# Where routing steps stand inside the slots of a two-layer hybrid block, and how the last rows are sent to their experts

## What is computed

```python
x = x + attention(layernorm(x))   # q = elu(x Wq)+1, k = elu(x Wk)+1, v = x Wv, H = 64
                                  # S_t = S_{t-1} + k_t v_t^T ; z_t = z_{t-1} + k_t
                                  # o_t = S_t^T q_t / max(z_t.q_t, 1e-6) ; out = o Wo
x = x + ffn(layernorm(x))
x = x + mix(layernorm(x))         # prev_t = x_{t-1} + d prev_{t-1}, d = exp(-exp(decay))
                                  # out = sigmoid(r_in Wr^T) * ((v_in Wv^T) Wo^T), *_in from x and prev
x = x + ffn(layernorm(x))

def ffn(x):                       # 8 experts, 128 -> 512 -> 128, the best one per token
    probs = softmax(x @ router_W + router_b)
    e = argmax(probs)
    return probs[e] * (relu(x @ W1[e] + b1[e]) @ W2[e] + b2[e])
```

## Time and profile before

| | |
|---|---|
| median of three runs | 393.11 us (392.72 to 397.33) |
| the profiled execution | 397.11 us, of which the span of the trace is 395.2 us |
| granted TensorE clock, mean | 0.862 of full speed |
| attention slots, first expert stage | about 27 to 94 us, about 98 to 203 us |
| mix slots, second expert stage | about 203 to 285 us, about 285 to 386 us |
| TensorE, VectorE, POOL, ScalarE busy | 75%, 63%, 51%, 37% |

### The profile page before, as it was taken

The page is one execution under the profiler, slowest core; times in us unless marked ns, Lnnn a source line. Parts: engine busy times, 40 slices in busy tenths (PEclk is TensorE's granted clock), DMA queues, the critical chain, the costliest instruction groups (busy, mean ns, idle before and its releaser), DMA issues.

```text
span 395.2 us, 8901 instructions
## 1 busy us (share of the span) xinstructions
PE 296.7 (75%) x2097; PEld 258.3 (65%) x2097; DVE 250.0 (63%) x996; ACT 147.1 (37%) x413; POOL 201.3 (51%) x259
## 2 busy tenths in 40 slices
PE   2899999680599379999923989695089729999980
PEld 1367666450488279999912878574088629999980
DVE  4656788784388167877725579467248627777760
ACT  3545554211133024444414555724123203444430
POOL 5823517777345724555424152777734554445550
PEclk9999999986589669999985889977559957999996
DMA  7990000024446448876325000001645736877700
GB/s 206 240 165 4 1 2 28 29 56 141 118 129 178 108 113 221 218 209 191 81 76 138 2 0 2 27 27 43 169 136 148 186 66 179 227 205 199 188 19 0
DMA packets 42609, 44.21 MB, mean 112 GB/s; under 512 B 7120, under 2 KB 29905, under 8 KB 42560
## 3 DMA queue, kind: packets, MB, share of 16 engines
q10 hardware_dynamic: 11808, 20.71, 20.9%
q1 hardware_dynamic: 26176, 14.39, 15.7%
q0 software_dynamic: 4576, 8.54, 6.1%
HBM read 33.06 MB, written 11.53 MB: 113 GB/s over the span
## 4 chain that ended last, share of the span: by engine, by line
PE 38%; issue 27%; DVE 11%; SPq 7%; another core or an unknown queue 5%; POOL 5%; ACT 2%; DMA 2%; DVEq 1%; POOLq 0%; ACTq 0%
PE pair L1319 14%; PE pair L1305 11%; PE bank L1305 4%; PE pair L1246 2%; POOL sorted L453 2%; DVE hT L1017 2%; SPq L344 2%; PE pair L1247 2%; SPq L340 2%; PE pair L1264 2%; SPq L312 1%; DVE xsn L1001 1%; ACT xn L535 1%; DVEq L1006 1%
## 5 line engine op out<-in xcount | busy, mean ns | idle before, releaser
L1319 PE MATMUL pair<-w2s,hT 128*128 x624 | 89.0, 289 | 8.2 <-issue 7.6
L1319 PEld LDWEIGHTS pair<-w2s,hT 128*128 128x128 f32 x624 | 80.9, 203 | 10.4 <-issue 9.9
L453 POOL DMA_INDIRECT sorted<-rows,place x64 | 64.2, 1003 | 31.3 <-issue 17.8
L1305 PE MATMUL pair<-xsT,w1s 128*128 128x128 f32 x472 | 70.2, 288 | 0.8 <-issue 0.8
L1305 PEld LDWEIGHTS pair<-xsT,w1s 128*128 128x128 f32 x472 | 63.6, 205 | 1.2 <-issue 1.2
L459 POOL DMA_INDIRECT out<-ys,xs x39 | 38.0, 975 | 41.2 <-issue 26.4
L459 POOL DMA_INDIRECT x_mid<-ys,xs x39 | 38.0, 975 | 40.7 <-issue 23.4
L1017 DVE TENSOR_SCALAR hT<-pair,w1s 128x128 f32<-128x128 f32 x156 | 47.1, 343 | 8.6 <-remote 3.9
L1028 DVE SCALAR_TENSOR_TENSOR ys<-pair,xs 128x128 f32<-128x128 f32 x78 | 27.2, 349 | 25.7 <-remote 13.0
L1009 DVE SCALAR_TENSOR_TENSOR xs<-b2b,xs 128x128 f32<-128x128 f32 x78 | 27.4, 352 | 21.4 <-DVE xsn L1001 14.6
L646 ACT COPY xsT<-bank 128x128 f32<-128x128 f32 x40 | 10.6, 265 | 67.4 <-PE bank L1296 27.4
(11 more groups left out here) (160 smaller groups left out, 505.5 us busy)
## 6 DMA issues: line engine op xcount, KB each, us to landing
w1s<-in_L_ffn_W_b ACTq DMA_DIRECT2D x78, 258.0 KB
xs<-sorted SPq DMA_DIRECT2D x78, 66.0 KB
rows<-in_L_attn_a_x SPq DMA_DIRECT2D x8, 256.0 KB, 4.9
w2s<-in_L_ffn_W SPq DMA_DIRECT2D x8, 256.0 KB, 5.5
rows<-x_mid SPq DMA_DIRECT2D x8, 256.0 KB, 4.8
sorted<-pad SPq DMA_DIRECT2D x30, 66.0 KB, 3.5
sorted<-rows,place POOLq DMA_INDIRECT x64
x_mid<-ys,xs POOLq DMA_INDIRECT x39
```

What stands on the lines that cost most here:

```text
L453: pool.indirect_dma_start(sorted_rows[l], bass.IndirectOffsetOnAxis(ap=place[:, t:t + 1], axis=0), rows[:, t, :], None).then_inc(s_sent[l] ...
L1305: mm = nc.tensor.matmul(bank[2 + 2 * half + i % 2][:, c * P:(c + 1) * P], w1s[i % NW][:, f:f + P], xsT[i % NB][:], start=True, stop=True)
L1319: mm = nc.tensor.matmul(bank[6 + i % 2][:, 0:P], hT[i % NB][:, c], w2s[:, bass.ds(e, 1), c, :].rearrange("p o d -> p (o d)"), start=(c == ...
```

## The change

The routing steps are the same instructions, in another order. In the attention slots VectorE does the places right after the mask instead of after the state, and the choice in front of the moments; POOL does the old logits in the middle of a group's four sends; ScalarE's exponentials move to the end of the slot. In the mix slots VectorE does places and choice in front of the moments, ScalarE's exponentials come at the end of the slot, a slot earlier (one more table load there), and TensorE counts in front of logits and mix. In the expert stages the last batch is chosen, counted and tabled earlier (2, 4, 5), and its eight sends are issued one per slot, behind the scatters of slots 4 to 11, instead of all after one scatter.

```diff
@@ -32,7 +32,7 @@
 
 STAGES = [(1, 9), (3, 8), (4, 22)]
 
-CHOOSE_AT, COUNT_AT, TABLE_AT = 3, 6, 6
+CHOOSE_AT, COUNT_AT, TABLE_AT = 2, 4, 5
 
 
 def after(eng, sem, n):
@@ -442,16 +442,24 @@
                 nc.gpsimd.tensor_tensor(lold[:, tiles(g)], kv[g % 2][:, :, H:VC], per_tile(std1[:, tiles(g)], GT),
                                         ALU.mult).then_inc(AS["lold"], 1)
 
-            def send(l, S, g):
-
+            def rows_ready(l, S, g):
                 b = batch_of(ROUTE_BATCHES, g)
                 pool.wait_ge(S["xnew"], g + 1)
                 pool.wait_ge(S["rs2"], 3 * (b + 1))
                 pool.wait_ge(s_gate[l], 2 * (b + 1))
                 pool.wait_ge(S["place"], b + 1)
-                for t in range(g * GT, (g + 1) * GT):
-                    pool.indirect_dma_start(sorted_rows[l], bass.IndirectOffsetOnAxis(ap=place[:, t:t + 1], axis=0),
-                                            rows[:, t, :], None).then_inc(s_sent[l][stage_of_batch(b)], 16)
+
+            def send_tile(l, t):
+                b = batch_of(ROUTE_BATCHES, t // GT)
+                pool.indirect_dma_start(sorted_rows[l], bass.IndirectOffsetOnAxis(ap=place[:, t:t + 1], axis=0),
+                                        rows[:, t, :], None).then_inc(s_sent[l][stage_of_batch(b)], 16)
+
+            def send(l, S, g, half=None):
+
+                if half != 1:
+                    rows_ready(l, S, g)
+                for t in range(g * GT + (GT // 2 if half == 1 else 0), (g + 1) * GT - (GT // 2 if half == 0 else 0)):
+                    send_tile(l, t)
 
             def scatter(l, i):
                 b = i % ND
@@ -462,11 +470,14 @@
                                         ).then_inc(s_sct[b], 16)
 
             def experts(l):
+                late = [t for g in ROUTE_BATCHES[LASTB] for t in range(g * GT, (g + 1) * GT)]
                 for i in range(ST):
                     scatter(l, i)
-                    if i == COUNT_AT - 1:
-                        for g in ROUTE_BATCHES[LASTB]:
-                            send(l, (AS, BS)[l], g)
+
+                    if i == COUNT_AT:
+                        rows_ready(l, (AS, BS)[l], LASTG)
+                    if COUNT_AT <= i < COUNT_AT + len(late):
+                        send_tile(l, late[i - COUNT_AT])
 
             def first_indirect():
 
@@ -487,9 +498,11 @@
                 if 0 <= k - 1 < NG:
                     z_dot_q(k - 1)
                 if k - 5 >= 0:
-                    send(0, AS, k - 5)
+                    send(0, AS, k - 5, 0)
                 if 0 <= k - 1 < NG:
                     old_logits(k - 1)
+                if k - 5 >= 0:
+                    send(0, AS, k - 5, 1)
             send(0, AS, 4)
             send(0, AS, 5)
             row_scales(AS, LASTB)
@@ -597,8 +610,6 @@
                 if k == NG:
                     for i in range(NW // 2):
                         load_w1(0, i)
-                if (b := batch_ending(ROUTE_BATCHES, k - 4)) is not None and b < LASTB - 1:
-                    lexp(0, AS, b)
                 if k + 1 < NG:
                     evac_xT(AS, k + 1, "vp")
                 if k + 2 < NG:
@@ -607,8 +618,8 @@
                     evac_v(k)
                 if 0 <= k - 1 < NG:
                     evac_o(k - 1)
-                if k == NG:
-                    lexp(0, AS, LASTB - 1)
+                if (b := batch_ending(ROUTE_BATCHES, k - 3)) is not None and b < LASTB:
+                    lexp(0, AS, b)
 
             def gates_of_mix(g):
                 act.wait_ge(BS["mix"], g + 1)
@@ -634,10 +645,10 @@
                 if k == NG:
                     for i in range(NW // 2):
                         load_w1(1, i)
-                if (b := batch_ending(ROUTE_BATCHES, k - 3)) is not None and b < LASTB:
-                    lexp(1, BS, b)
                 if 0 <= k - 1 < NG:
                     evac_x2T(k - 1)
+                if (b := batch_ending(ROUTE_BATCHES, k - 2)) is not None and b < LASTB:
+                    lexp(1, BS, b)
 
             def experts(l):
                 def evac_xs(i):
@@ -851,17 +862,17 @@
                     phi(k)
                 if 0 <= k - 1 < NG:
                     mask_scores(k - 1)
+                if (b := batch_ending(ROUTE_BATCHES, k - 4)) is not None and b < LASTB - 1:
+                    placed(0, AS, b)
                 if 0 <= k - 2 < NG:
                     add_attention(k - 2)
                 if 0 <= k - 1 < NG:
                     add_state(k - 1)
-                if (b := batch_ending(ROUTE_BATCHES, k - 4)) is not None and b < LASTB - 1:
-                    placed(0, AS, b)
+                if (b := batch_ending(ROUTE_BATCHES, k - 3)) is not None and b < LASTB:
+                    choose(0, AS, b)
                 if 0 <= k - 2 < NG:
                     dve.wait_ge(AS["xnew"], k - 1)
                     moments(AS, 2, k - 2)
-                if (b := batch_ending(ROUTE_BATCHES, k - 3)) is not None and b < LASTB:
-                    choose(0, AS, b)
                 if k < NG:
                     scan_z(k)
                 if k == NG:
@@ -901,15 +912,15 @@
                     add_mix(k - 1)
                 if k + 1 < NG:
                     scan_mix(k + 1)
+                if (b := batch_ending(ROUTE_BATCHES, k - 3)) is not None and b < LASTB:
+                    placed(1, BS, b)
+                if (b := batch_ending(ROUTE_BATCHES, k - 2)) is not None and b < LASTB:
+                    choose(1, BS, b)
                 if 0 <= k - 1 < LASTG:
                     dve.wait_ge(BS["xnew"], k)
                     moments(BS, 2, k - 1)
                 if k + 4 < NG:
                     first_moments(1, k + 4)
-                if (b := batch_ending(ROUTE_BATCHES, k - 3)) is not None and b < LASTB:
-                    placed(1, BS, b)
-                if (b := batch_ending(ROUTE_BATCHES, k - 2)) is not None and b < LASTB:
-                    choose(1, BS, b)
                 if k == NG - 1:
                     slot_table(1, 0)
 
@@ -1269,12 +1280,12 @@
             def mix_slot(k):
                 if k + 1 < NG:
                     transpose_x(BS, k + 1)
+                if (b := batch_ending(ROUTE_BATCHES, k - 3)) is not None and b < LASTB:
+                    count(BS, b, bank[7])
                 if 0 <= k - 2 < NG:
                     logits(k - 2)
                 if k < NG:
                     mix(k)
-                if (b := batch_ending(ROUTE_BATCHES, k - 3)) is not None and b < LASTB:
-                    count(BS, b, bank[7])
                 if 0 <= k - 1 < LASTG:
                     transpose_x2(k - 1)
```

## The result

The changed kernel takes 400.85 us (median of 4 runs, 398.41 to 405.1) against 393.54 us before (4 runs): the ratio is 1.0149, 95% interval 1.0101 to 1.0197. The forecast was 383.0 us, faster; the kernel came out 1.5% slower. The trace of the changed kernel is of the execution of 405.1 us, 4 us above its median and the slowest of the four, so I compare stretches and orders in it, and let the ratios carry the sizes.

What follows compares the result with a forecast made beforehand. POOL's back-to-back indirect DMAs were taken to hold up TensorE in the expert stages, and POOL to set the pace before them. -2.7 + 0.6 - 8.0 = -10.1 us (-4.0 per layer in expert stages) gave 383.0 us, range 375 to 394.

Steps and rivals of the forecast that it cites:

- The bound and the hold: Expert stages: back-to-back indirect DMAs of POOL hold up TensorE's word where SP issues too; about 10 us lost per layer.
- Attention, -2.7 us: Attention slots: earlier places start POOL's sends 1.8 us sooner and save a 1.4 us wait, less 0.5.
- Mix, +0.6 us: Mix slots: table loads make batch 0's place about 1.8 us later; a 1.19 us wait absorbs all but 0.6.
- Slots 0 to 4, +2.5 us: Expert stages: earlier choice, count and places, with 0.5 us waiting for the count, move slot 4's ys from 121.64 to 124.1.
- Slots 4 to 12 at 3.3 and then 2.53 us: Expert stages: four slots at 3.3 us while SP issues fills, then four at 2.53; slot 12's ys at 147.4, before 151.4.
- It wants the rows at 152. Enough: Slot 17, expert stage: last send lands near 148, SP loads by 150, rows wanted at 152, so no loss.
- Rival 3: Slots 4 to 11: each pair holds TensorE to its full tail, 5.0 us a slot, +12.7 per layer, 416 us; chance 0.10.

Runs made afterwards that it cites:

- e7: Kernel before, with a small unused power on POOL behind each of the last batch's eight sends, so they start 2.3 us apart: ratio 1.0082, 397.63 us.
- f2: Kernel before, with a small unused add on POOL behind the last batch's sends and the scatters from slot 6, 1.5 us apart: ratio 0.9957, 396.12 us.
- e4: Kernel before, with SP's eight fills issued only after the last batch's sends have landed: ratio 1.0057, 396.11 us.
- Session B: The two groups of timed runs without the hold, where the kernel before took 369 us.
- g1: Kernel before, with the last batch's eight sends in two runs of four, behind the scatters of slots 5 and 7: ratio 1.0121.
- session A: The three groups of timed runs with the hold, where the kernel before took 394 to 397 us.
- e1: Changed kernel with the expert stages of before, so only the attention and mix slots differ from before: ratio 0.9995, 393.34 us.

## Why the prediction was wrong

- **The bound and the hold: right in the main.** POOL's spacing sets the hold (e7, and f2 in part), and e4 takes SP out of the reading. With POOL's sends at 2.3 instead of 1.27 us the slots 6 to 13 went from 3.7 to 2.3 us each. The Trainium skill (SBUF — State Buffer, "SBUF: two separate sides"), by which DMAs slow no compute, does not cover this. Session B is as it says (slots 6 to 13 take 2.2 us each in g1 beside a run at 1.28 us); in session A the measurement decides.
- **Attention, -2.7 us: right mechanism, somewhat too large.** The waits for places fell from 4.72 to 2.87 us and from 1.42 to 0.17 us, as forecast; but two sends of the four grew to 1.88 and 1.75 us behind the old logits. From POOL's second z product to the stage's last send it is 72.2 to 73.5 us in the nine traces of session A with the old slots, and 70.7 to 71.5 in the four with the new: about -2 us.
- **Mix, +0.6 us: not told from nothing.** From slot 38's ys to the next layer's slot 0 it is 94.4 to 96.4 us with the old order and 95.3 to 96.2 with the new. The two together, -1.4 us, lie inside e1's interval (-1.6 to +1.2 us).
- **Slots 0 to 4, +2.5 us: right in layer 0, too small in layer 1.** 2.7 and 3.8 us measured. The wait for the count, put at 0.5 us, was 2.74 us on TensorE, for the mask `oh` of the choice in front of it.
- **Slots 4 to 12 at 3.3 and then 2.53 us: failed in its second half.** They took 25.8 and 26.9 us, 3.2 and 3.4 us a slot, where 23.3 were forecast, and the last four were as slow as the first (12.7 against 13.1 us in layer 0). Within a pair, and from a pair to the next where ys is there, POOL's DMAs are still 1.27 us apart, and the hold is there in pieces (waits for "remote" of up to 3.88 and 4.55 us). POOL waits only once TensorE is late.
- **"It wants the rows at 152. Enough": failed, and by itself enough to take the whole gain.** The last send started at 148.97, as forecast within 1 us (its landing was put near 148), but SP's first load only at 152.19, not by 150, and the rows were normalised at 154.46. Slot 17's rows are wanted by its `norm_rows`, which stands three slots ahead, ahead of slot 14's ys on VectorE. In the kernel before that is 7.3 us ahead of its ys; with the ys forecast at 156.8 it makes 149.5, and not 152. And from the last send to the first load it is 3.2 us, then 2.3 more to the first instruction that has the rows. With the last send at the forecast 148 that gives 153.5, which is when the kernel before normalises them (153.49): no gain in layer 0, even at the forecast pace.

Expert stages, loss (+) or gain (-) in us against the kernel before:

| | forecast, each layer | layer 0 | layer 1 |
|---|---|---|---|
| slots 0 to 4 | +2.5 | +2.7 | +3.8 |
| slots 4 to 12 | -6.4 | -3.9 | -2.8 |
| slots 12 to 16 | 0 | +3.4 | +5.1 |
| behind slot 16 | 0 | 0.0 | +1.4 |
| sum | -4.0 | +2.2 | +7.5 |

So 17.7 us lie between forecast and trace. The waits for rows are 4.6 of them (1.51 and 3.09), the pace of slots 4 to 13 is 9.5 (6.1 up to slot 12, 3.4 in slot 13). The two steps hang together: a faster pace alone would have met the rows missing, rows in time alone would have met held slots; neither alone gives the forecast, or even a gain in the expert stages. (The medians of the two kernels, 7.3 us apart, are nearer than these two traces.) No rival named the gate. Rival 3 gave the right sign: pairs do hold TensorE, but not to its 5.0 us a slot. Its border, "above 3.8 us a slot", is 3.4 by its own numbers ((151.4 - 124.1) / 8), and the pace measured lies at or under it.

## What to carry to other kernels

Before work is spread out, look for who waits for its **last** piece. Spreading shortens the local stall and delays the end, and a consumer that waits for all pieces pays for that delay as soon as the stall no longer covers it. Read its need at the first instruction that touches the data, not at the last. And when a releaser named by the profile ended well ahead of the start, look for another one that ended just ahead of it.

An idle stretch put down to "remote" may belong to the session, not the kernel: an edit that helps only by shortening it should be timed again at another time.

## What the runs showed of the hardware

- POOL's indirect DMAs at 1.27 us held TensorE's word back in session A, until 1.8 to 2.0 us behind the end of the run's last DMA (1.4 and 1.5 in e7, behind its nine scatters); at 1.5 us the hold was 1 to 2 us shorter; at 2.3 us there was none; in session B there was none even at 1.28. The kernel before took 397.0 us and 369.2 us on chips of the same number.
- In the hold SP is slow too. Its register instructions ahead of the fills (duration in ns, min/median/max) in the changed kernel's trace of session A, then of session B:

```profile
L303 SPq FUSED_REGOPS  x16: 16/37/719, 123.7 to 320.6; - x16
```

```profile
L303 SPq FUSED_REGOPS  x16: 37/37/42, 118.4 to 310.2; - x16
```

An instruction that touches no data takes up to 0.72 us instead of 0.04. That suggests that what is slow in the hold is common to the engines' sequencers, but no run isolates it. What it is, and what sets the session, no run here shows either.
